# Layer 2 of a four-layer graph network: the transposed features come from V by four 128x128 transposes, and heads 2 and 3 are turned one tile later

## The reference, cut to what matters

```python
def _gat_layer(h, mask, b):
    scores = jnp.einsum('...nd,...md->...nm', h, h)
    scores = jnp.where(mask, scores, NEG)
    attn = jax.nn.softmax(scores, axis=-1)
    return jnp.einsum('...nm,...md->...nd', attn, h) + b

h = jnp.einsum('bnc,hdc->bhnd', x, Wh)            # four heads, 64 channels each
out_h = _gat_layer(h, mask[None, None], bh[None, :, None, :])
cat = jnp.transpose(out_h, (0, 2, 1, 3)).reshape(B, N, H * D)
z = jax.nn.leaky_relu(cat, negative_slope=0.2)
h2 = jnp.einsum('bnk,dk->bnd', z, Wo)             # the output layer
out2 = _gat_layer(h2, mask[None], bo)
z2 = jax.nn.leaky_relu(out2, negative_slope=0.2)
# then a layer norm of z2 with gamma and beta
```

## Time and profile before

| what | value |
|---|---|
| runs | 2188.56, 2191.05, 2191.91 us; median 2191.05 us |
| profiled execution, own time | 2190.72 us |
| its span, first to last instruction | 2188.3 us |
| mean granted TensorE clock | 0.977 of full |
| busy share of the span: PE / PEld / DVE / ACT / POOL | 90% / 71% / 79% / 53% / 45% |
| the chain that ended last, by engine | PE 70%, DVE 14%, POOL 7%, issue 4%, ACT 3% |

### The profile page before, as it was taken

The page is one execution under the profiler, slowest core; times in us unless marked ns, Lnnn a source line. Parts: engine busy times, 40 slices in busy tenths (PEclk is TensorE's granted clock), DMA queues, the critical chain, the costliest instruction groups (busy, mean ns, idle before and its releaser), DMA issues.

```text
span 2188.3 us, 94465 instructions
## 1 busy us (share of the span) xinstructions
PE 1966.7 (90%) x43592; PEld 1562.7 (71%) x43592; DVE 1729.5 (79%) x2148; ACT 1164.8 (53%) x1404; POOL 987.9 (45%) x683
## 2 busy tenths in 40 slices
PE   1788768999999999999999999999999999947898
PEld 1677758996777777777777777777777777736777
DVE  1799879987778878888787887887877877737998
ACT  1344333424666666666666666666666666623332
POOL 1676488852234424344243343442434433326663
PEclk9999979999999999999999999999999999978999
DMA  7000000001111111111111111111111111100101
GB/s 164 3 3 4 3 2 2 2 2 31 32 32 32 32 34 29 39 30 36 32 30 33 32 31 32 32 32 32 32 35 30 35 34 29 27 10 8 27 23 32
DMA packets 88250, 61.19 MB, mean 28 GB/s; under 512 B 45616, under 2 KB 86832, under 8 KB 87856
## 3 DMA queue, kind: packets, MB, share of 16 engines
q1 hardware_dynamic: 85632, 54.57, 10.3%
q10 hardware_dynamic: 2224, 0.59, 0.2%
HBM read 8.98 MB, written 4.19 MB: 6 GB/s over the span
## 4 chain that ended last, share of the span: by engine, by line
PE 70%; DVE 14%; POOL 7%; issue 4%; ACT 3%; SPq 1%; DMA 1%; DVEq 0%; POOLq 0%; ACTq 0%
PE ACC L1175 30%; PE S L1285 24%; DVE ring L895 5%; PE AX L1344 4%; PE AX L1328 3%; PE S L1264 3%; DVE ring L1019 3%; ACT ring L752 2%; PE AX L1305 2%; POOL EV_both L583 1%; PE AX L1155 1%; POOL ln_rstd L453 1%; PE S L1223 1%; SPq L396 1%; DVE ch_rden L1004 1%
## 5 line engine op out<-in xcount | busy, mean ns | idle before, releaser
L1019 DVE TENSOR_TENSOR ring<-ring,mask_self_t 128x1024 f32<-128x1024 f32 x640 | 897.9, 1412 | 265.1 <-ACT ring L752 264.4
L1175 PEld LDWEIGHTS ACC<-V,ring 128*64 128x64 f32 x28672 | 961.3, 138 | 191.4 <-DVE ring L895 39.3
L1175 PE MATMUL ACC<-V,ring 128*64 128x65 f32 x28672 | 986.3, 223 | 38.2 <-issue 19.5
L752 ACT ACTIVATE ring<-S,dot_bias 128x1024 f32<-128x1024 f32 x640 | 713.2, 1114 | 436.5 <-PE S L1285 402.4
L1285 PE MATMUL S<-FA 128*64 128x512 f16 x5120 | 666.5, 382 | 7.4 <-DMA FA<-lo 7.0
L1285 PEld LDWEIGHTS S<-FA 128*64 128x64 f16 x5120 | 255.6, 110 | 214.5 <-ACT ring L752 54.1
L895 DVE SCALAR_TENSOR_TENSOR ring<-S,pair_q,mask_t 128x1024 f32<-128x1024 f32 x256 | 317.5, 1272 | 0.2 <-issue 0.2
L583 POOL TENSOR_TENSOR EV_both<-score,recip 128x512 f32<-128x512 f32 x64 | 124.3, 1943 | 426.0 <-DVE score L1026 426.0
L1264 PE MATMUL S<-parts,mask_t 128*128 128x128 bf16 x3072 | 180.9, 223 | 29.9 <-DVE X L1008 18.3
L1264 PEld LDWEIGHTS S<-parts,mask_t 128*128 128x128 bf16 x3072 | 179.2, 100 | 32.2 <-issue 29.7
L445 POOL TENSOR_TENSOR ln_xc<-X,ln_mean 128x512 f32<-128x512 f32 x64 | 72.8, 1137 | 208.8 <-DVE ln_mean L879 208.3
(11 more groups left out here) (111 smaller groups left out, 1789.2 us busy)
## 6 DMA issues: line engine op xcount, KB each, us to landing
FA<-hi SPq DMA_DIRECT2D x320, 64.0 KB, 2.1
FA<-lo SPq DMA_DIRECT2D x320, 64.0 KB, 2.1
X<-in_x SPq DMA_DIRECT2D x16, 256.0 KB, 5.4
EV_both<-in_adj SPq DMA_DIRECT2D x8, 512.0 KB, 4.3
out_x<-X SPq DMA_DIRECT2D x16, 256.0 KB, 2.6
wh<-in_wh_t ACTq DMA_DIRECT2D x2, 64.0 KB, 4.7
bh_bc<-in_bh ACTq DMA_DIRECT2D x1, 128.0 KB, 5.1
w_gat<-in_w_gat ACTq DMA_DIRECT2D x4, 16.0 KB, 4.1
```

Of the source, the lines that this page charges most:

```text
L752: act.activation(ring[:, jt, :], S[jt % 2][:, :], ACT.Exp, bias=dot_bias[:, n % 2:n % 2 + 1])\
L1019: dve.tensor_tensor(ring[:, jt, :], ring[:, jt, :], mask_self_t[:, jt, :], ALU.mult)\
L1175: last = pe.matmul(acc_of(t)[rows, :], ring[:, jt, t * P + c * CUT:t * P + (c + 1) * CUT], values, start=(jt == 0 and t % 4 == 0), stop=(j ...
```

## The change: what it does

1. `features` no longer multiplies weights and inputs. It transposes the values of the same unit with four 128x128 transposes into the same bank, and waits for `v_copied`, which ACT raises when it has copied them to SBUF.
2. ACT copies the values into a new buffer `v_by_pair` (128 x 512, one for all units), in an order of 64-channel blocks such that a 128-column block holds node tile q and node tile q + 4. It now does so ahead of the squares and waits for `v_made`, by which POOL says that it has read the buffer for the unit before.
3. POOL's bias add reads `v_by_pair` and writes `V`; before it worked in `V` in place.
4. `turn_heads(b - 1, 1)` on PE moves from jt 5 to jt 6 of head 0. ACT's copy of its result stays at jt 6.

The pieces are, in order: the new buffer, POOL's and ACT's `values`, PE's `features` and `dot_unit`.

```diff
+        v_by_pair = sb("v_pairs", [P, TD])
+        v_pairs = v_by_pair[:, :].rearrange("p (q h d) -> p h q d", q=T // 2, h=2)
...
             def values(u):
-                own = V[:, u["n"] % 3, :, 1:D + 1]
                 bias = bo_bc[:, :] if u["kind"] == "out" else bh_bc[:, u["h"], :]
                 pool.wait_ge(v_copied, u["n"] + 1)
-                pool.tensor_tensor(own, own, chans(bias), ALU.add).then_inc(v_made, 1)
+                pool.tensor_tensor(halves_of(V[:, u["n"] % 3, :, 1:D + 1]), v_pairs, halves_of(chans(bias)), ALU.add)\
+                    .then_inc(v_made, 1)
...
+                wait(act, v_made, u["n"])
+                act.activation(v_pairs, V_FULL, ACT.Copy).then_inc(v_copied, 1)
                 act.activation(sq[:, :].rearrange("p (h n) -> p h n", h=2), AX_both[:, :, 0:T // 2 * D], ACT.Square)\
                     .then_inc(sq_made, 1)
-                act.activation(halves_of(V[:, u["n"] % 3, :, 1:D + 1]), V_FULL, ACT.Copy).then_inc(v_copied, 1)
...
             def features(u):
-                out_unit = u["kind"] == "out"
-                chunks = range(2 if out_unit else 1)
+                pe.wait_ge(v_copied, u["n"] + 1)
                 k = take_bank(AX_AT["F", u["n"]])
-                for i in chunks:
-                    for half in range(2):
-                        own = slice(half * D, (half + 1) * D)
-                        if out_unit:
-                            rows, w = z_t[:, i, half * HALF:(half + 1) * HALF], wo[:, i, :]
-                        else:
-                            rows, w = h_t[own, u["b"] % 2, :], wh[own, u["h"], :]
-                        last = pe.matmul(AX[k][own, :], w, rows, start=(i == 0), stop=(i == chunks[-1]),
-                                         skip_group_check=True)
+                for q in range(T // 2):
+                    last = pe.transpose(AX[k][:, q * P:(q + 1) * P], v_by_pair[:, q * P:(q + 1) * P], ident[:, :])
                 last.then_inc(ax_full[k], 1)
...
-                if jt == 5 and is_head(u, 0) and b > 0:
+                if jt == 6 and is_head(u, 0) and b > 0:
                     turn_heads(b - 1, 1)
```

## The result

| | before | changed |
|---|---|---|
| median of 4 runs | 2191.48 us | 2128.79 us |
| range | 2188.56 to 2192.89 | 2126.66 to 2129.04 |
| profiled execution, own time | 2190.72 us | 2128.7 us |
| its span | 2188.3 us | 2126.9 us |
| ratio to before | | 0.9713, 95% interval [0.9702, 0.9725] |

The forecast was 2127.0 us with a range of 2117 to 2143: right in direction, in mechanism and, by 1.7 us (profiled execution against profiled execution), in size.

A forecast was written before the change was run, and what follows sets the result against it. PE was taken to bound the kernel. Features of heads 26.2, of out units 15.5, the last unit 0.8 and the moved turn 21.2 sum to 63.7 us, taking 2190.7 to 2127.0 us, range 2117 to 2143.

The forecast's parts named there:

- PE is the bound: Layer 2: PE busy 87.09 of 89.15 us per batch, so time taken from its queue comes off the end.
- Features of a head, 0.41 us: PE's features in heads: four transposes at 0.69 us replace 1.10 us, saving 0.41 us, 26.2 us for 64 heads.
- Features of an out unit, 1.03 us: PE's features in out units: 0.69 us replaces 1.72 us, saving 1.03 us, 15.5 us for 15 in the loop.
- The last unit, 0.82 us: The 16th out unit, after idle time: four transposes at 1.12 us replace products at 1.94 us, saving 0.82 us.
- The moved turn, 21.2 us: Head 0 turn, one tile later: 1.79 us of PE work covers the 1.41 us wait, saving 21.2 us over 15.
- The new waits: PE waiting for `v_copied` and ACT for `v_made`: both claimed to cost zero.
- POOL's add: POOL's bias add reading another buffer: 0.2 us less to 1 us more, claimed to cost zero.
- the copy's order: ACT's copy ahead of the squares: squares come 0.5 us later, claimed to cost zero.
- The head 3 wait stays: Head 3 turn: PE and the chain to norm_all both move by 0.41 us, so the 0.73 us wait stays.
- A waiting turn: Rival: the moved head 0 turn still waits, 2148 us with all the wait left, 2138 with half; chance 0.08.
- no overlap: Rival: PE's feature transposes do not overlap, 1.09 us a block plus 0.10 for the switch, 2167 us; chance 0.03.
- the clock: Rival: full-array transposes lower PE's granted clock, up to 2245 us at 3 us of each unit; chance 0.03.

The follow-up runs named there:

- the out-units kernel: The changed kernel with transposes for the out units alone, heads having their two products back: 2153.29 us, ratio 0.9822 to the kernel before.
- part 1 alone: The changed kernel with the turn in head 0 back at jt 5, so only the transposed features remain: 2151.21 us, ratio 0.9815 to the kernel before.
- both turns late: The changed kernel with the turn in head 3 moved from jt 5 to jt 6 too: 2118.20 us, ratio 0.9665 to the kernel before.
- the transposes twice: The changed kernel with the four feature transposes issued twice into the same places: 2161.56 us, ratio 0.9861 to the kernel before.
- part 2 alone: The kernel before with only the turn in head 0 moved from jt 5 to jt 6: 2170.44 us, ratio 0.9903 to the kernel before.
- the add done twice: The changed kernel with POOL's bias add done twice, the second after the first: 2129.97 us, ratio 0.9720 to the kernel before.
- the squares first: The changed kernel with ACT's squares ahead of its copy of the values: 2127.47 us, ratio 0.9705 to the kernel before.

## Why the prediction was right

- **PE is the bound.** Shown. PE's queue lost 2.77 us of work a batch (87.09 to 84.32) and the 1.34 us wait, and the batch lost 4.10; a second add on POOL cost nothing, 0.43 us more on PE cost 0.42 us each.
- **Features of a head, 0.41 us.** Shown in start-to-start times, to 0.01 us; the sum over 64 came 2 us short by the runs of the out-units kernel. 1.0 of these 2 us is the DMA wait below, which the profiled execution of the changed kernel had and that of the out-units kernel did not. The first of the 64 gave its share like the others: from the start of its values block to the first `dots` it was 14.18 us before (492.18 to 506.36) and is 13.75 us now (492.40 to 506.15), although the wait for ACT ahead of its transposes grew from 1.39 to 1.51 us. (The prediction counts 31 blocks of eight in the trace; the 256 transposes of the earlier trace rows make 32. Nothing rests on it.)
- **Features of an out unit, 1.03 us.** Right at the block (1.72 against 0.10 + 0.59). The `dots` after it takes 0.89 us start to start (1028.72 to 1029.61), where it took 0.87 (1230.37 to 1231.24); this 0.02 was left out, 0.3 us in all.
- **The last unit, 0.82 us.** This term of the sum was wrong: nothing of it arrived. From the start of its values block to its first `dots` it was 14.07 us (1921.75 to 1935.82) and is 14.06 us (1860.22 to 1874.28). The features did end sooner: it is 0.86 us less from their start to the copy of `hi`. But they started 0.11 us later, behind a wait for ACT of 1.45 instead of 1.34 us, and of the DMA issues behind, one took 1.34 us (from 1867.60) where it took 0.60 before (from 1929.88): 0.11 and 0.74 us take back the 0.86. The same place took 1.34 us with part 1 alone and 1.47 with both turns late, but 0.60 in the six others. Long issues are not peculiar to this place, nor to the change. Of the 640 issues that send features in layer 2, 46 took 1.0 us or more in the kernel before and 60 in the changed one (46 and 50 in the two kernels without any transposed features, 55 to 66 in the seven with them). In the loop nearly all of them pass without a wait of PE; in the last unit PE has nothing else to run. What lengthens an issue, and whether the change makes it more frequent, was not tested.
- **A term left out: the way of the features into `dots`.** The prediction let the features end sooner and took for granted that the DMAs of `hi` and `lo` are in `FA` when the next unit's `dots` come. Once in the changed kernel they were not. PE's timeline, and the chain that led there:

```profile
612.39 1.05 PE L1288 MATMUL S<-FA 128*64 128x512 f16 x8 [1.01 <-DMA FA<-lo]
```

```profile
604.55 1.84 SPq L412
...
608.59 3.77 DMA FA<-lo
```

  One issue took 1.84 us, and the last transfer landed 3.77 us after its issue, where the median of its kind is 2.1. The kernel before had one such wait inside its loop, of 0.15 us (at 1685.73). The nine traces have 14 such waits in the loop, between none (out units alone) and 1.8 us in all (the transposes twice), and each stands less than 12 us behind an issue that took 1.07 us or more. So long issues cost time in the loop too, by chance as far as is known; no experiment varied them.
- **The moved turn, 21.2 us.** Shown by part 2 alone (20.7) and by part 1 alone, where it comes back as 16 waits. The cover of 1.79 us was enough, by 0.35 us.
- **The new waits, POOL's add, the copy's order: nothing.** Shown by the add done twice and the squares first; no wait of PE for `v_copied` or of ACT for `v_made` stands in the loop. After the moved turn ACT's exp still waits for PE and not for ACT's two copies, as worked out: it starts 0.40 us after them (at 1020.13).
- **The head 3 wait stays.** Right, at 15 x 0.73 us, and the experiment with both turns late shows that it was there for the taking, by the same move.
- **The rivals.** A waiting turn, no overlap and the clock are each ruled out by a row above, and neither a cheaper block nor a shorter wait in head 3 came to help. For the clock: the Trainium skill (TensorE: Matmul & The Clock Gate, Part 4: PE-mode transpose) says that the full clock does not engage for transposes. Blocks of four between other products left the granted clock at 1.00 from 560 to 1840 us (0.99 from 506 to 1890 us, as before the change), and blocks of eight at the 1.00 shown above; a stretch of transposes alone was not run. The 275 ns that the prediction sets beside its 273 ns are of 16-bit data (bf16) on that page, while this kernel transposes 32-bit data: that the two agree is not a check of the one by the other.

The forecast was 63.7 us. The span of the profiled execution became 61.4 us shorter (2188.3 to 2126.9), 2.3 us less than that. Its own time fell by 62.0 us because the time outside the span was 1.8 instead of 2.4 us, which has nothing to do with the change: 0.6 us of the good fit is luck. Where the 2.3 us are can be read from the traces. From the values block of the first unit to that of the last it was 1429.57 us and is 1367.82 us, 61.75 less, where the prediction has 26.2 + 15.5 + 21.2 = 62.9. The DMA wait (1.01 against 0.15 us) and the 0.02 us after each out unit (0.3) are this difference. The last unit is 0.8. The first values block stood 0.2 us later (492.40 against 492.18), before any changed instruction; the kernel before and part 2 alone, with the same program up to there, differ by 1.6 us (492.18 and 490.57). The last 0.1 us went behind layer 2's last unit.

## What to carry to other kernels

When one engine's queue is full, price an edit from start to start against a block of the same shape and neighbours that the trace already has, switch of array shape included (here four records of 273 ns make 1.09 us, and the block took 0.59). A wait that the profile shows ahead of a block in a full queue goes away if the block moves behind as much other work as the wait is long, as long as you follow the releasing chain, see how much of it the same edit shortens, and check that the reader of the block's result comes late enough. And take all such waits at once: the same one-line move in head 3 was worth another 10.6 us. Look at the rare waits too: one of 0.15 us for a DMA was the only sign, inside the loop of the kernel before, of what cost the changed one 1.0 us.

## What the runs showed of the hardware

- 128x128 transposes of 32-bit data: 273 ns for one record, but 0.59 us for four and 1.02 us for eight between products of another shape, so 0.11 us for each further one.
- Going from 64-column products to full-array transposes costs 0.10 us ahead of the block (1.03 instead of 0.93 us for the sums), for `v_pairs` as for `ln_y` and the turns.
- A mask on DVE beside POOL's additions takes 2.15 us instead of 1.23. It is a matter of overlap: a second add that reached 0.43 us into a pair of masks cost the pair 0.29 us.
- A DMA issue on SP of this kernel's features mostly takes 0.46 or 0.60 us, but 46 to 66 of the 640 in a trace took 1.0 to 2.1 us, in all nine traces. Few cost anything: PE waited for the transfers 14 times in the loops of the nine traces, by 0.15 to 1.02 us, and a long issue stands in the last unit, where PE has no other work, in four of them. What lengthens them stayed open.
